# One direct group in place of two: group 1 computed in seven products, its work interleaved with group 0's outputs

## What is computed

```
x = x + (x @ W[cat[b]] + bias[cat[b]])                 # layer 0: 256 -> 256, weights chosen by batch
s0 = relu(x @ swi[0]) @ swo[0]                         # two shared MLPs, 256 -> 1024 -> 256
s1 = relu(x @ swi[1]) @ swo[1]
eo = relu(x @ wi[type[b]]) @ wo[type[b]]               # an MLP chosen by batch
w  = softmax(relu(concat(eo[:,0], s0[:,0], s1[:,0]) @ g1) @ g2)     # from the first token only
x  = x + eo*w0 + s0*w1 + s1*w2
```

## Time and profile before

| | |
|---|---|
| median of 3 runs | 269.25 us |
| the profiled execution | 269.19 us, its span 267.4 us |
| PE busy | 262.8 us, 98% |
| PEld | 217.4 us, 81% |
| DVE | 160.6 us, 60% |
| ACT | 150.3 us, 56% |
| POOL | 163.3 us, 61% |
| granted TensorE clock | 9 tenths or more in all 40 slices |

### The profile page before, as it was taken

The page is one execution under the profiler, slowest core; times in us unless marked ns, Lnnn a source line. Parts: engine busy times, 40 slices in busy tenths (PEclk is TensorE's granted clock), DMA queues, the critical chain, the costliest instruction groups (busy, mean ns, idle before and its releaser), DMA issues.

```text
span 267.4 us, 3466 instructions
## 1 busy us (share of the span) xinstructions
PE 262.8 (98%) x1160; PEld 217.4 (81%) x1160; DVE 160.6 (60%) x245; ACT 150.3 (56%) x266; POOL 163.3 (61%) x172
## 2 busy tenths in 40 slices
PE   7999999999999999999999999999999999999995
PEld 7688888888888888888888888888888888888884
DVE  2777968735644444655345575345476577985664
ACT  2587457775665655665645644546545764645320
POOL 0379999999948949927945725626626528535000
PEclk9999999999999999999999999999999999999999
DMA  4844322012022012112022012022022022000404
GB/s 139 257 154 159 118 78 80 14 68 80 2 78 78 5 74 78 37 46 78 0 78 81 9 69 81 0 81 78 2 78 78 0 78 67 13 0 0 156 4 157
DMA packets 7473, 18.31 MB, mean 68 GB/s; under 512 B 1312, under 2 KB 2080, under 8 KB 7456
## 3 DMA queue, kind: packets, MB, share of 16 engines
q1 hardware_dynamic: 6592, 16.65, 18.8%
q10 hardware_dynamic: 864, 1.44, 1.6%
HBM read 16.00 MB, written 2.10 MB: 68 GB/s over the span
## 4 chain that ended last, share of the span: by engine, by line
PE 96%; DMA 2%; SPq 1%; issue 0%; DVE 0%; ACT 0%; DVEq 0%
PE acc L730 48%; PE chain L730 23%; PE right L730 12%; PE left L730 6%; PE acc L739 4%; DMA w_raw<-cat_w 2%; SPq L237 1%; PE left L782 1%; PE chain L782 1%; PE corner L730 1%; PE right L782 1%; PE corner L782 1%; SPq L239 0%; DVE x L721 0%; ACT w_hi L375 0%
## 5 line engine op out<-in xcount | busy, mean ns | idle before, releaser
L281 POOL TENSOR_TENSOR m_lo<-staged,m_hi 128x512 fp32r<-128x512 f32 (+2 forms) x49 | 82.9, 1702 | 67.2 <-ACT m_hi L363 63.1
L730 PE MATMUL acc<-h_hi,m_hi 128*128 128x512 f32 x190 | 73.9, 389 | 0.0
L730 PE MATMUL acc<-h_lo,m_hi 128*128 128x512 f32 x190 | 73.9, 389 | 0.0
L730 PE MATMUL acc<-h_hi,m_lo 128*128 128x512 f32 x190 | 73.9, 389 | 0.0
L387 ACT COPY kept<-chain 128x512 f32<-128x512 f32 x66 | 38.8, 588 | 54.1 <-PE chain L730 54.0
L730 PEld LDWEIGHTS acc<-h_hi,m_lo 128*128 128x128 f32 x190 | 35.7, 188 | 7.5
L730 PEld LDWEIGHTS acc<-h_hi,m_hi 128*128 128x128 f32 x190 | 35.7, 188 | 7.4
L730 PEld LDWEIGHTS acc<-h_lo,m_hi 128*128 128x128 f32 x190 | 35.7, 188 | 7.3
L518 DVE SCALAR_TENSOR_TENSOR h_lo<-left,h_hi 128x512 fp32r<-128x512 f32 x24 | 16.6, 691 | 28.4 <-ACT h_hi L399 28.4
L281 POOL TENSOR_TENSOR staged<-staged 128x128 f32<-128x128 f32 x66 | 31.4, 490 | 1.7
L523 DVE TENSOR_TENSOR left<-left,kept 128x512 f32<-128x512 f32 x22 | 15.3, 695 | 24.3 <-PE left L730 24.3
(11 more groups left out here) (149 smaller groups left out, 437.2 us busy)
## 6 DMA issues: line engine op xcount, KB each, us to landing
staged<-mlp_w SPq DMA_DIRECT2D x22, 512.0 KB, 3.4
x<-x_t ACTq DMA_DIRECT2D x4, 256.0 KB, 4.1
x<-x_t SPq DMA_DIRECT2D x4, 256.0 KB, 7.3
out_t<-x SPq DMA_DIRECT2D x2, 512.0 KB, 4.7
staged<-mlp_w SPq DMA_DIRECT2D x3, 256.0 KB, 3.6
g_sb<-g SPq DMA_DIRECT2D x1, 768.0 KB, 3.8
out_t<-x SPq DMA_DIRECT2D x3, 256.0 KB, 2.3
w_raw<-cat_w SPq DMA_DIRECT2D x4, 128.0 KB, 2.9
```

Source lines behind the costliest of these rows:

```text
L281: return nc.gpsimd.tensor_tensor(out, a, b, ALU.subtract)
L730: last = nc.tensor.matmul(out[:, columns], half[:, slot, at:at + P], moving[:, columns], start=(start and n == 0), stop=(stop and n == 2), ...
```

## The change

Group 1 is computed in seven products as all later groups are (`DIRECT = 1`), and `direct` is gone. On PE layer 0 of batch 1 follows group 0's direct products at once; then group 1's products come with group 0's outputs between them, as in the later groups. So group 1 needs its sums S1 to S4 and the sums t1 to t4 of x, and the orders of all queues are rewritten:

- SP loads batch 1's layer 0 weights and x(1,0) before the expert number is read; x(1,1) comes behind group 1, which is now one load of 512 KB. Group 2's load waits for group 0's first part (POOL) and for wo of group 0 being split.
- ACT waits for the first part of x(0,0) before it issues x(0,1).
- POOL computes t1, t2 before x_lo of tile (1,0), and t3, t4 behind; then m_lo of group 1 in two parts. It no longer splits wo of group 0.
- DVE takes group 1's weight sums (`weight_sums`) and the low part of wo of group 0, and t1, t2's low parts come earlier.

```diff
-DIRECT = 2
+DIRECT = 1
@@ semaphores
+        wo_loaded = sem("wo_loaded")
+        wo_hi_ready = sem("wo_hi_ready")
+        wo_split = sem("wo_split")
@@ numbering of m_hi's and m_lo's parts
         def first_part(j):
-            return j + 1 if j < DIRECT else 2 * j + 1
+            return 2 * j if j else 1
         def second_part(j):
-            return DIRECT + j + 1 if j < DIRECT else 2 * j + 2
+            return 2 * j + 1
@@ SP
             load_layer0(0)
+            load_layer0(1)
+            for d in range(DC):
+                load_x(sp, 1, 0, d)
...
-                    if j >= 2:
+                    if j == 2:
+                        sp.wait_ge(m_split, first_part(0))
+                        sp.wait_ge(wo_split, 1)
+                    elif j > 2:
                         sp.wait_ge(m_split, second_part(j - 2))
                     load_group(sp, bank, j)
                     if j == 1:
-                        for t in range(HALVES):
-                            for d in range(DC):
-                                load_x(sp, 1, t, d)
-                        load_layer0(1)
+                        for d in range(DC):
+                            load_x(sp, 1, 1, d)
@@ POOL
+            def split_parts(j):
+                raw = staged[:, j % 2, :]
+                pool.wait_ge(m_hi_ready, first_part(j))
+                subtract(m_lo[:, j % SLOTS, 0:PLAIN], raw[:, 0:PLAIN], m_hi[:, j % SLOTS, 0:PLAIN].bitcast(F32)).then_inc(m_split, 1)
+                pool.wait_ge(m_hi_ready, second_part(j))
+                subtract(m_lo[:, j % SLOTS, S1:SPLIT], raw[:, RAW_S:RAW], m_hi[:, j % SLOTS, S1:SPLIT].bitcast(F32)).then_inc(m_split, 1)
...
-            split_first(1, False)
+            pool.wait_ge(x1_ready, 4)
+            first_sums(0)
             for d in range(DC):
                 pool.wait_ge(x_hi_ready[1], d + 1)
                  subtract(x_part(x_lo, 1, 0, d), x1_part(1, 0, d), x_part(x_hi, 1, 0, d).bitcast(F32)).then_inc(x_split[1][0][d], 1)
-            split_first(0, True)
-            split_first(1, True)
-            pool.wait_ge(x1_ready, 4)
-            pair_sums(0)
-            for j in range(DIRECT, N):
+            last_sums(0)
+            split_parts(1)
+            for j in range(2, N):
                 split_group(j)
@@ ACT
             load_x(act, 0, 0, 1)
+            act.wait_ge(x_loaded[0][0][0], 16)
             for d in range(DC):
                 load_x(act, 0, 1, d)
...
             part_hi_of(2)
-            split_first_hi(1, False)
-            hidden_hi(0, 0)
-            x_hi_of(1, 0, 0)
-            hidden_hi(0, 1)
-            x_hi_of(1, 0, 1)
-            hidden_hi(0, 2)
-            split_first_hi(0, True)
-            hidden_hi(0, 3)
             for d in range(DC):
+                x_hi_of(1, 0, d)
                 w_hi_of(1, d)
-            split_first_hi(1, True)
+            for n in range(2):
+                t_hi_of(0, n)
             for d in range(DC):
                 x_hi_of(1, 1, d)
+            split_hi(1)
             for i in range(4):
-                hidden_hi(1, i)
-            for n in range(4):
+                hidden_hi(0, i)
+            act.wait_ge(wo_loaded, 16)
+            nc.scalar.copy(m_hi[:, 0, WO:A11], staged[:, 0, WO:A11]).then_inc(wo_hi_ready, 1)
+            split_hi_sums(1)
+            for n in range(2, 4):
                 t_hi_of(0, n)
-            split_hi(DIRECT)
-            split_hi_sums(DIRECT)
             for j in range(DIRECT, N):
                 keep(j, 0)
@@ DVE
+            def weight_sums():
+                raw = staged[:, 1, :]
+                dve.wait_ge(staged_loaded[1], 16)
+                a11, a12, a22, a21 = (raw[:, at:at + P] for at in (A11, A12, A22, RAW_A21))
+                s1, s2, s3, s4 = (raw[:, RAW_S + i * P:RAW_S + (i + 1) * P] for i in range(4))
+                nc.vector.tensor_tensor(s1, a21, a22, ALU.add).then_inc(sums_ready, 1)
+                subtract(s3, a11, a21).then_inc(sums_ready, 1)
+                dve.wait_ge(sums_ready, 1)
+                subtract(s2, s1, a11).then_inc(sums_ready, 1)
+                dve.wait_ge(sums_ready, 3)
+                subtract(s4, a12, s2).then_inc(sums_ready, 1)
...
-            for i in range(4):
-                hidden_lo(0, i)
             for d in range(DC):
                 w_lo_of(1, d)
+            for i in range(2):
+                t_lo_of(i)
             for d in range(DC):
                 x_lo_of(1, 1, d)
+            for i in range(2):
+                hidden_lo(0, i)
+            weight_sums()
             dve.wait_ge(bias_loaded[1], 16)
             make_x1(1, 0, 0)
-            hidden_lo(1, 0)
+            hidden_lo(0, 2)
+            dve.wait_ge(wo_hi_ready, 1)
+            subtract(m_lo[:, 0, WO:A11], staged[:, 0, WO:A11], m_hi[:, 0, WO:A11].bitcast(F32)).then_inc(wo_split, 1)
+            hidden_lo(0, 3)
             make_x1(1, 0, 1)
-            for i in range(1, 4):
-                hidden_lo(1, i)
             make_x1(1, 1, 0)
             make_x1(1, 1, 1)
-            for i in range(4):
+            for i in range(2, 4):
...
@@ PE
-                if u == 0 and j < DIRECT:
-                    pe.wait_ge(m_split, second_part(j))
+                if u == j == 0:
+                    pe.wait_ge(wo_split, 1)
...
             direct_first()
-            for j in range(1, DIRECT):
-                for i in range(4):
-                    direct(j, i)
             for t in range(HALVES):
                 layer0(1, t)
-            for u in range(8):
-                output(0, u)
             for j in range(DIRECT, N):
                 product(j, 1)
                 product(j, 2)
```

More of the change, by code:

```diff
@@ L125, in build @@
         staged_loaded = [sem(f"staged_loaded{i}") for i in range(2)]
-        wo_loaded = [sem(f"wo_loaded{i}") for i in range(DIRECT)]
+        wo_loaded = sem("wo_loaded")
+        wo_hi_ready = sem("wo_hi_ready")
+        wo_split = sem("wo_split")
         g_loaded = sem("g_loaded")
@@ L197, in load_group @@
             if j < DIRECT:
-                if j:
-                    load_wi(eng, bank, j)
-                eng.dma_start(staged[:, j % 2, WO:A11], group_weights(bank, j, slice(WO, A11))).then_inc(wo_loaded[j], 16)
+                eng.dma_start(staged[:, j % 2, WO:A11], group_weights(bank, j, slice(WO, A11))).then_inc(wo_loaded, 16)
             else:
@@ L300, in split_group, with first_sums @@
                 subtract(s4, a12, s2).then_inc(sums_ready, 1)
[L301 to L304, removed]
+                split_parts(j)
             def pair_sums(pair):
-                (b, t), (c, u) = PAIRS[pair]
-                t1, t2, t3, t4 = (t_raw[:, i, :] for i in range(4))
                 if pair:
                     pool.wait_ge(t_split, 4 * pair)
+                first_sums(pair)
+                last_sums(pair)
+            def first_sums(pair):
+                (b, t), (c, u) = PAIRS[pair]
+                t1, t2 = t_raw[:, 0, :], t_raw[:, 1, :]
                 subtract(t1, x1_part(c, u, 0), x1_part(b, t, 0)).then_inc(t_ready, 1)
@@ L314, in pair_sums, with last_sums @@
                 subtract(t2, x1_part(c, u, 1), t1).then_inc(t_ready, 1)
+            def last_sums(pair):
+                (b, t), (c, u) = PAIRS[pair]
+                t2, t3, t4 = (t_raw[:, i, :] for i in range(1, 4))
                 subtract(t3, x1_part(c, u, 1), x1_part(c, u, 0)).then_inc(t_ready, 1)
@@ L349, in _ @@
         def _(act):
[L350 to L356, removed]
             def split_hi(j):
@@ L623, in x_lo_of, with t_lo_of @@
                 subtract(x_part(x_lo, b, t, d), x1_part(b, t, d), x_part(x_hi, b, t, d).bitcast(F32)).then_inc(x_split[b][t][d], 1)
+            def t_lo_of(i):
+                dve.wait_ge(t_hi_ready, i + 1)
+                subtract(t_lo[:, 0, i, :], t_raw[:, i, :], t_hi[:, 0, i, :].bitcast(F32)).then_inc(t_split, 1)
+            def weight_sums():
[9 more added lines that the diff above has]
+                subtract(s4, a12, s2).then_inc(sums_ready, 1)
             nc.vector.memset(ones[:], 1.0).then_inc(ones_ready, 1)
@@ L643, in _ @@
             part_lo_of(2)
-            for i in range(4):
-                hidden_lo(0, i)
             for d in range(DC):
                 w_lo_of(1, d)
+            for i in range(2):
+                t_lo_of(i)
             for d in range(DC):
                 x_lo_of(1, 1, d)
+            for i in range(2):
+                hidden_lo(0, i)
+            weight_sums()
             dve.wait_ge(bias_loaded[1], 16)
             make_x1(1, 0, 0)
-            hidden_lo(1, 0)
+            hidden_lo(0, 2)
+            dve.wait_ge(wo_hi_ready, 1)
+            subtract(m_lo[:, 0, WO:A11], staged[:, 0, WO:A11], m_hi[:, 0, WO:A11].bitcast(F32)).then_inc(wo_split, 1)
+            hidden_lo(0, 3)
             make_x1(1, 0, 1)
-            for i in range(1, 4):
-                hidden_lo(1, i)
             make_x1(1, 1, 0)
             make_x1(1, 1, 1)
-            for i in range(4):
```

(4 more changed lines are left out.)

## The result

The changed kernel takes **278.77 us** (median of six runs, 277.64 to 280.94), the kernel before 269.25 (268.95 to 269.69): a ratio of 1.0365, 95% interval 1.0343 to 1.0388. The profiled execution took 277.83, with a span of 276.0 and a mean clock of 0.992.

A forecast was written before the change was run, and what follows sets the result against it. TensorE, busy 98% of the span, was taken as the bound. Three matmuls saved (-0.68), waits up to output 0 (+7.03) and product 7's stall (+2.2) gave +8.55: 277.8 us, own range 276.6 to 279.5, widened to 275.0 to 280.5.

The forecast's parts named there:

- output 0: Group 0's first output on PE, waiting for wo's residue on DVE: forecast at 31.88 in place of 24.85.
- product 7: Group 1's seventh product on PE, waiting for ACT's keep(1,1) behind group 2's load: forecast at 36.8, stall 2.2.
- The turns: POOL and DVE operations reading two SBUF tensors block each other and alternate: 1.70 us a pair, 1.43 with 256 DVE columns.
- the turns bite little: Rival: POOL and DVE do not block each other or blocks fall elsewhere, DMA sets the pace; 271.9 us, chance 0.13.
- The stalls: PE's waits from part_lo(2) through batch 1's layer 0 to group 1's products: 0.3, 1.0, 0.5, 2.3, 2.0, 2.2 us.
- The weight sums: DVE's four sums of 128x128 before wo's residue: 0.22 us each, 0.9 in all, bounds 0.15 and 0.47 each.
- The start: Shift of the copies before t1 because ACT holds x(0,1,*) back: taken as 0, bounds -0.4 and +0.7 us.
- The id load: SP's load of ids between batch 1's loads: 4.5 us by an earlier row, its delay expected to stay hidden.
- POOL's split of group 2: POOL's sums and split for group 2 end at about 39.3, before PE wants them at 42.9: slack.
- The clock: PE's granted clock through the pauses: forecast to stay at 1.00; a rival had it fall, 279.8 us, chance 0.18.
- a sign against itself: The forecast called itself wrong if, among other signs, PE's clock leaves 1.00.
- the rival's +2.0: Rival that the clock falls: slow matmuls from output 0 on add 2.0 us, giving 279.8; chance 0.18.

The follow-up runs named there:

- e2: Changed kernel with six of DVE's low parts of batch 1 reading one operand from PSUM (values not the true ones): 276.03 us.
- e1: Changed kernel with ACT's copy m_hi of group 2, which waits for that group's load, moved behind group 1's kepts: 276.68 us.
- e5: Changed kernel with the PSUM operands of e2 and the ACT order of e1 together: 272.92 us.
- e6: Kernel before with one line of the change alone, ACT's wait for the first part of x(0,0): 268.97 us, ratio 0.9991.
- e3: Changed kernel with four short matmuls on zeros in each of two PE pauses of 2 us: 278.01 us.
- e8: Changed kernel's complete computation with the POOL, DVE and ACT queues around group 1 in another order: 270.72 us, ratio 1.0080.
- e4: Changed kernel with the ACT order of e1 and the zero matmuls of e3 together: 276.65 us.

## Why the prediction was right

| step | forecast | measured |
|---|---|---|
| layer 0 of batch 1 starts | 19.32 | 19.09 |
| POOL's first part of m_lo(1) ends | 26.1 | 25.77 |
| product 1 | 28.49 | 28.22 |
| wo's residue ends | 31.83 | 31.60 |
| output 0 | 31.88 | 31.70 |
| group 2's load issued, landed | 32.0, 35.3 | 31.82, 35.18 |
| product 7 | 36.8 | 36.77 |
| group 2's first product (+8.55 or +8.60) | 42.92 | 42.97 |

The steps agree to 0.35 us or better, and the mechanism is the forecast's. That 277.83 and 277.8 agree to 0.03 is luck, as the points below say.

- **The turns** carried the sum. Pairs that no row of before showed (w_lo and t_lo against x_lo and t1 to t4) cost what other pairs had shown, 1.70 for 512 and 1.43 for 256 columns. e2 shows the cause and rules out *the turns bite little*: the transfers would have allowed far less, x(1,1,*) having landed at about 17.5 and 18.2.
- **The stalls.** Forecast 0.3, 1.0, 0.5, 2.3, then 2.0 and 2.2; the idle times are 0.15, 0.73, 0.27, 1.96, 1.86 and 0.64. A row's idle time leaves out the tail of the matmul before it, so starts are the better measure. e1 and e5 show that the last is ACT's order.
- **The weight sums** were taken at 0.22 each between 0.15 and 0.47; their step is 0.23.
- **The start**, taken as 0 between -0.4 and +0.7, was -0.28, which is no more than single executions differ by (e6). Of that 0.18 was left at output 0 and 0.03 at product 7: small errors of the other sign used it up.
- **The id load**, 4.5 by the row of before, took 2.6. It was hidden, so the error cost nothing. POOL's split of group 2 ended at 40.41 and not at 39.3; PE wanted it at 42.97, so this cost nothing either.
- **The clock** is where the forecast was wrong: it was said to stay at 1.00 and it fell, which the text had named as a sign against itself. In the profiled execution the fall cost nothing (e3), so the rival's +2.0 didn't come either: the fall lay wholly ahead of product 7 and left no slow matmul behind it. But it stood behind pauses of 1.96 and 1.86 us. The Trainium skill, "TensorE: Matmul & The Clock Gate", section "HAM oscillation — how this bites in real kernels", tells of waits of some 3 to 5 us; here the clock fell behind 1.96 and 1.86 us, with ten matmuls between them.
- **The median**, which is what was forecast, lies 0.97 above the forecast and 0.94 above the profiled execution whose steps the table has. No term of the sum stands for this. Mean clocks of the six runs are 0.986 to 0.994 (e1, with one fall in its profile, has 0.994), so several of them had more than one fall or a longer one. But 277.64 and 279.61 both have 0.988: the clock explains the spread in part at most. Something else lengthens single executions at full clock, with this change or without it: 273.46 in e6 (median 268.97), 276.81 in e2 (profiled 274.05) and the four of e8, all at 0.999 or 1.000. None of these was profiled, and the cause is open.

## What to carry to other kernels

Before a saving on the bound engine is counted, add up what its producers must do by the new due time; if two of them share something that lets only one work at a time, as POOL and DVE with two SBUF inputs each, add their times as if they were one engine (in e8 about 10.5 us of work for 10.6 us). A load that comes a little late costs what stands behind its first reader in a strict queue, not what needs the load: put the reader last. A profiled execution can lie at the lower edge of the runs, so a forecast made on its rows should be set against the spread, above all where the change brings pauses to an engine that had none.

## What the runs showed of the hardware

- A DVE operation with one operand in PSUM isn't held by POOL and doesn't hold it: POOL's t3 and t4 took 1.30 and 1.29 in e2, and 1.48 and 1.73 in the changed kernel.
- Weight sums of 128x128, which alone step at 0.23, are held in e2: the first takes 0.90, with POOL's 512 columns under way, the second 2.19 beside its 896 columns, the last two 0.60 together, when POOL is through: a short operation pays for what is left of the other engine's.
- The TensorE clock fell to half behind pauses of about 2 us: 1.96 and 1.86 in the changed kernel, in e1 already behind one of 1.94. It need not fall: e2 has 0.83, 1.62 and 2.20 at a clock of 1.00. Short matmuls on zeros in two of these pauses, eight in the trace of each, went with no fall in the profile of e3 and with one in that of e4, while three other runs of e4 show 0.999 and 1.000.
